# When the row maxima and the ranks of large counts are worked out on VectorE

## The reference, cut to what matters

```python
x = x + _L0_gnn_ref(_layernorm(x), edge_weight, L0_gnn_bias, edge_index)     # scatter-built 1024x1024 weight
x = x + _L0_ffn_ref(_layernorm(x)[None], wg, w1, b1, w2, b2)[0]              # 8 experts, top 2, capacity 314
x = x + _L1_gnn_ref(_layernorm(x), edge_index, L1_gnn_W, L1_gnn_b)           # degree-normed sum over 41250 edges
x = x + _L1_ffn_ref(_layernorm(x)[None], L1_ffn_w1, L1_ffn_w2)[0]            # 1024 -> 4096 -> 1024, ternary weights
```

## Time and profile before

| | before |
|---|---|
| median of 3 runs | 1056.78 us (1055.4 to 1057.2) |
| span of the profiled execution, first to last instruction | 1054.4 us |
| TensorE busy | 979.3 us, 93% |
| VectorE busy | 737.9 us, 70% |
| ScalarE busy | 467.1 us, 44% |
| chain that ended last | PE 74%, DVE 14%, issue 6%, DMA 3% |
| mean granted TensorE clock | 0.977 |

### The profile page before, as it was taken

How to read it: one execution, slowest core, us unless ns; L and a number is a source line. 1 busy time by engine, 2 the same in 40 slices (tenths; PEclk the granted TensorE clock), 3 DMA queues, 4 the chain that set the end, 5 groups by cost and what they waited for, 6 DMA issues and landing times.

```text
span 1054.4 us, 17446 instructions
## 1 busy us (share of the span) xinstructions
PE 979.3 (93%) x6781; PEld 533.9 (51%) x6781; DVE 737.9 (70%) x1038; ACT 467.1 (44%) x573; POOL 128.0 (12%) x139
## 2 busy tenths in 40 slices
PE   1799899996899999999969999899999999999998
PEld 0688655553555666665534444444444444444444
DVE  7999888877664555668679754999977555555541
ACT  5344446553355565566522113999733122222221
POOL 6300042320311111000043100011000000000000
PEclk9899899998899999999989999999999999999999
DMA  3800026665778898885446855788513554444441
GB/s 121 243 2 2 2 81 227 244 228 193 233 293 306 324 350 323 318 320 204 159 162 182 215 128 178 278 319 310 186 40 71 120 120 113 109 109 109 110 98 36
DMA packets 166145, 188.91 MB, mean 179 GB/s; under 512 B 126520, under 2 KB 126842, under 8 KB 161984
## 3 DMA queue, kind: packets, MB, share of 16 engines
q1 hardware_dynamic: 159679, 165.47, 49.1%
q0 software_dynamic: 6400, 22.55, 6.5%
HBM read 137.98 MB, written 35.33 MB: 164 GB/s over the span
## 4 chain that ended last, share of the span: by engine, by line
PE 74%; DVE 14%; issue 6%; DMA 3%; ACT 2%; POOL 0%; DVEq 0%; SPq 0%; ACTq 0%; POOLq 0%
PE ps L1095 20%; PE ps L1293 13%; PE ps L1322 12%; PE ps L1202 8%; PE ps L1218 6%; DVE fq L2276 3%; PE ps L1275 2%; PE ps L1159 2%; DMA eo_d<-eo 2%; DVE w1l L2111 2%; PE ps L982 1%; PE ps L955 1%; DVE stats L1775 1%; PE ps L973 1%; DVE o_key L1854 1%
## 5 line engine op out<-in xcount | busy, mean ns | idle before, releaser
L1293 PE MATMUL ps<-w1q,xqt 128*128 128x512 fp8e4 x640 | 139.9, 379 | 0.4 <-issue 0.4
L1656 ACT ACTIVATE hf<-ps,fs 128x512 f32<-128x512 f32 x80 | 54.9, 688 | 183.2 <-PE ps L1293 183.2
L1322 PE MATMUL ps<-w2q,hqt 128*128 128x512 fp8e4 x576 | 126.4, 379 | 0.0
L2360 DVE TENSOR_REDUCE hm<-hf 128x1 f32<-128x512 f32 x80 | 54.2, 685 | 73.8 <-ACT hf L1656 73.8
L1293 PEld LDWEIGHTS ps<-w1q,xqt 128*128 128x128 f16 x640 | 62.4, 98 | 75.8 <-issue 0.9
L1322 PEld LDWEIGHTS ps<-w2q,hqt 128*128 128x128 f16 x576 | 56.3, 98 | 66.9
L1095 PE MATMUL ps<-wt_h,xt 128*128 128x512 f16 x320 | 85.4, 379 | 0.0
L1095 PE MATMUL ps<-gwt_h,xt 128*128 128x512 f16 x320 | 84.5, 379 | 0.6 <-issue 0.6
L1202 PE MATMUL ps<-xdh,w1h 128*128 128x314 f16 x256 | 77.1, 301 | 6.2 <-ACT ht L1566 3.3
L1202 PE MATMUL ps<-xdh,w1l 128*128 128x314 f16 x256 | 76.4, 299 | 0.0
L1202 PE MATMUL ps<-xdl,w1h 128*128 128x314 f16 x256 | 76.3, 298 | 0.0
(11 more groups left out here) (320 smaller groups left out, 1949.5 us busy)
## 6 DMA issues: line engine op xcount, KB each, us to landing
wstage<-in_L_ffn_w SPq DMA_DIRECT2D x32, 1024.0 KB, 10.9
abs_in<-in_L_ffn_w SPq DMA_DIRECT2D x18, 1024.0 KB, 6.5
abs_e<-in_L_ffn_w SPq DMA_DIRECT2D x14, 1024.0 KB, 5.1
fnat_b<-in_L_ffn_w SPq DMA_DIRECT2D x28, 512.0 KB, 6.4
fnat_a<-in_L_ffn_w SPq DMA_DIRECT2D x27, 512.0 KB, 4.8
eo_d<-eo SPq DMA_DIRECT2D x16, 512.0 KB, 3.1
hq_d<-hq SPq DMA_DIRECT2D x8, 1024.0 KB, 6.3
xs_d<-xs_all SPq DMA_DIRECT2D x10, 512.0 KB, 2.9
```

The source lines that it names most:

```text
L1293: last = mm(ps[:, n % 4, :], xqt[:, u, k, :], w1q[:, k // 2, n * 512:(n + 1) * 512, k % 2], start=(k == 0), stop=(k == KD - 1))
L1322: last = mm(ps[:, 4 + h, :], hqt[:, u, k, :], w2q[:, k // 2, h * 512:(h + 1) * 512, k % 2], start=(k == 0), stop=(k == KF - 1))
L1656: cp(hf[:, i % 2, n * 512:(n + 1) * 512], ps[:, n % 4, :], ACT.Gelu, scale=fs[:, i % 2, 3:4]).then_inc(s_ge, 1)
L2360: last = v.tensor_reduce(hm[:, u, n:n + 1], hf[:, u, n * 512:(n + 1) * 512], AX.X, ALU.max, apply_absolute_value=True)
```

## The change

The maxima of tiles 7, 8 and 9 move from the end of expert 6 to a place before the first expert, right after `dinv` is done. VectorE's `ranks()`, which stood after the second eviction of the last expert, moves behind the sixth and last one. TensorE's list, and those of the other engines, stay as they are.

```diff
@@ last_expert
                     result_rows(e, ep, n // 2, n % 2)
                     w1_part(n)
                     w1_low(2 + n)
-                    if n == 1:
-                        ranks()
                 result_rows(e, ep, 2, 0)
                 result_rows(e, ep, 2, 1)
+                ranks()
                 for i in range(4, KD):
                     w1_part(i)
                     if i + 2 < KD:
@@ expert
                 low_rows(e)
                 if isinstance(e, int):
-                    for b in range(NE - 1, NT):
-                        low_rows(b)
                     dve.wait_ge(s_cmax, NT)
                     v.tensor_scalar(cflag[:, :], cmax[:, :], EXACT, None, ALU.is_ge).then_inc(s_cflag, 1)
@@ ahead of the experts
             dve.wait_ge(s_dinv2, 2)
+            for b in range(NE - 1, NT):
+                low_rows(b)
 
             pairs(dve, expert, NE)
```

## The result

| comparison | before, median | changed, median | ratio, 95% interval |
|---|---|---|---|
| the result (8 runs each) | 1055.45 us | 1059.87 us (1055.48 to 1062.81) | 1.0041, 1.0024 to 1.0058 |
| repeated as run e3 (35 and 12 runs) | 1055.32 us | 1057.81 us (1056.60 to 1064.64) | 1.0031, 1.0008 to 1.0055 |

What follows compares the result with a forecast made beforehand. PE, busy 93% of the span, was taken as the bound. Terms -0.65, -0.46, +1.46, +0 and +1.5 sum to +1.85 us: span 1056.25, plus 2.4 to the median, 1058.6 us, range 1056.3 to 1060.4.

Steps and rivals of the forecast that it cites:

- A: The forecast itself: PE's tail waits for `sel` and the clock falls; 1058.6 us, from 1057.7 to 1059.8, chance 0.53.
- The waits on `htl`: Last expert's group (0,0): two PE waits vanish as three maxima leave the end of expert 6; -0.65 us.
- The gap in `w1_t(3)`: Last expert: without ranks before eviction (1,0), `gwt_l` is copied in time and PE runs through; -0.46 us.
- Expert 0: Three maxima ahead of expert 0 stay hidden behind PE's group (0,0), about 0.3 us to spare; 0, bounds 0 and +0.4.
- The tail outlasts the gathers: After the last expert, `ranked(0)` waits for `sel`, so PE's tail delays `mixed`; +1.46 us, whole change net +0.35.
- The clock: PE's tail: 3.2 us idle before `ranked(0)` lowers the granted clock to half; +1.5 us, bounds 0 and 1.76.
- rival C: Maxima delay expert 0 by 0.4 us and the slow clock costs the tail 3.5 us; 1061.0 us, chance 0.12.
- Rival B: The tail waits for `sel` but PE keeps its full clock; +0.35 us, 1057.1 us, chance 0.17.
- Rival D: DVE bounds the last expert and its 6.3 us relief counts; 1050.5 us, chance 0.06, half 1055.7, chance 0.04.
- E: The tail's cover is wider than read, gain and loss cancel, no effect; 1056.8 us, chance 0.08.

Runs made afterwards that it cites:

- e3: The changed kernel run again, unaltered, for a second trace and its spread: 1057.81 against 1055.32 us before, ratio 1.0031.
- e6: The changed kernel with three more maxima ahead of expert 0 (tiles 7 to 9 again, into unused words): 1062.88 against 1055.13 us before, ratio 1.0084.
- e4: The changed kernel with 14 unused matmuls filling TensorE's idle stretch ahead of the first ranked matmul: 1054.89 us, ratio 0.9985 of before.
- e10: The changed kernel with 14 matmuls in TensorE's idle stretch, repeated on one chip with e11: 1055.21 us, ratio 1.0004 of before.
- e11: The changed kernel with 7 matmuls in TensorE's idle stretch, repeated on one chip with e10: 1056.00 us, ratio 1.0009 of before.
- e1: The kernel before with only the three maxima moved ahead of expert 0, ranks left in place: 1054.0 against 1055.32 us, ratio 0.9985.
- e12: Only the three maxima moved, against the kernel before, a repeat of e1: 1055.45 against 1054.91 us, ratio 1.0011.
- e2: The kernel before with only the ranks moved behind the sixth eviction, maxima left in place: 1057.5 against 1055.32 us, ratio 1.0015.
- e8: The changed kernel, unaltered, a third execution traced for the clock of its tail alone: that execution took 1060.31 us.
- e5: The changed kernel with the ranks split into two halves behind the last expert's first and second copies: 1055.69 against 1055.13 us before, ratio 1.0001.
- e9: e5 with the loads of gnat 4 and 6 issued before SyncE's waits for evictions and stores: 1052.73 against 1054.91 us before, ratio 0.9984.
- e7: The changed kernel with 7 unused matmuls in TensorE's idle stretch ahead of the first ranked matmul: 1056.96 against 1055.13 us before, ratio 1.0020.

## Why the prediction was right, and what was mis-sized

The time, 1059.87 us, lies in the range, on the side of slower, and the mechanism of A is what the traces show. That the number fell into the range is in part luck. The sum was built on a median of before of 1056.78 us from 3 runs, which became 1055.45 from 8. On that base it gives 1057.3 and its range 1055.0 to 1059.1, and 1059.87 lies outside. The change was predicted as +1.85 us and came out as +4.4 in the first medians and +2.5 in the repeat. By its steps:

- **The waits on `htl`, -0.65.** From group (0,0) to `w1_t(0)` it was 3.28 us before (14.08 to 17.36) and is 2.59 after (14.20 to 16.79): -0.69. Right in size. The two waits were at the second and the fourth quarter (500.92 and 502.56 before), not at the third and fourth as the prediction has it.
- **The gap in `w1_t(3)`, -0.46.** From `w1_t(3)` to `w1_t(4)` 4.16 us before, 3.70 after. Right, and the evictions come 1.15 us earlier from group (0,0) on (18.29 against 19.44), against 1.11.
- **Expert 0, 0.** 28.9 us in before and in all traces with three maxima. Right. The spare time at the fourth quarter was 0.9 us and not 0.3: counted from expert 0's first matmul, `htl(3)` started at 14.32 rather than 14.80 us. With more maxima it is the first quarter that waits (e6), which the prediction didn't look at.
- **The tail outlasts the gathers, net +0.35.** In the three fills without a slow stretch or a late copy (e4, e10, e11) the second `mixed` comes 32.68 to 32.69 us after group (0,0), before 32.38: +0.31. Right against this one trace of before. But before ends in a gather, and behind the same gather e1 took 32.34 and e12 30.57 us, so in other executions the net can be about 1 us larger or smaller.
- **The clock, +1.5.** This is the term whose range was too narrow. Behind the same idle PE lost 0 (e2), 1.32 (result), 1.42 (e8), 1.69 (e6) and 2.86 us (e3). I had set the upper bound at 1.76, one slow stretch as in expert 1; that a second could follow while PE was busy I had only as a part of rival C. In the changed kernel's own three traces the mean is 1.9, and the late copy on ScalarE, for which the sum has no term, adds 0.33, 0.12 and 0. The prediction quotes the Trainium skill ("TensorE: Matmul & The Clock Gate", section "HAM oscillation — how this bites in real kernels") as if its rule held for any wait; the section tells it of a kernel in which every burst is shorter than the wait for a transfer behind it. In the wide form e2's trace, 3.27 us of idle and a clock of 1.00 behind it, goes against it.

From (0,0) to the second `mixed` those three traces lost 1.96, 3.17 and 1.84 us, 2.3 in the mean, against 1.85 predicted. The medians say 4.4 and 2.5, ratios 4.3 and 3.3. The second agrees with the traces within its interval (0.8 to 5.8 us); the first, with its lower end at 2.5, only at the edge. What more there was in those eight runs isn't settled. The traced execution of them was the second shortest, so the others may have lost more in the tail; another candidate is the late transfer of e8, which is not tied to the change by any run here, and executions of before also reach 1062.59 us.

Rival B (no clock loss) is what e2's trace shows, with the ranks alone; no trace with both parts moved shows it. Rival C had the longer slow stretch right in kind (e3) and the 0.4 us at expert 0 wrong; 1059.87 lies between its 1061.0 and A's 1058.6, a little above A's own upper end of 1059.8, so the median alone wouldn't choose between them. Rival D falls with e1 and e5: with 4.2 us of maxima gone nothing comes out in the time, and with the ranks hidden as well the loads bind. The maxima were on the chain for 5.58 us and were worth 0.7 to PE. E falls with the intervals.

## What to carry to other kernels

A block of small instructions moved off one engine's critical place has a reader somewhere, and its cost is the reader's: look up in the reader's list what stands behind the wait and whether that list ends at the same barrier. Count the idle that the new wait gives TensorE twice, once as time and once as a stretch at the half clock that may follow; here the tail outlasting the gathers came to some 1.5 us and the slow stretch to 1.3 to 2.9. And when an engine is relieved and nothing comes of it, look for the transfers that were issued behind its work: a gain clear of before was measured only in e9, after two of them had been moved too.

## What the runs showed of the hardware

- The same idle ahead of the same work is answered differently from one execution to the next: after 3.26 or 3.27 us the granted clock stayed 1.00 in e2 and fell to 0.50 in the three traced executions of the changed kernel and in e6 (0.50 from 526 to 528), in one of them (e3) for twice as long.
- The length of the idle doesn't order the cases: after 2.52 us in e6 the clock fell, after 2.88 us in e8 it did not (1.00 from 602.5 to 606); after 1.75 and 1.76 us (e11, e7) it did not.
- A slow stretch can go on while PE is busy all the time: 521.5 to 524.7 in e3, busy 3.20 of 3.20 us at 0.50.
- The way over the last store and the gathers varies by 2 us: from the last evictions to the second `mixed` 11.7 us (e9), 11.8 (e12), 12.7 (e5), 12.9 (before) and 13.6 (e1). In e1 and e12, the same kernel, it is 13.6 and 11.8.
